# A post-norm decoder layer on one Trainium2 core: banks, splits and transposes in another order

## What is computed

```python
x = layernorm(x + gated_slot_attention(x, Wq, Wk, Wv, Wg, Ws, Wo, g_norm_weight))
x = layernorm(x + cross_attention(q=x, k=ctx_512, v=ctx_512))
g = (x @ gate_w.T) * gate_s          # [2048, 1408]
u = (x @ up_w.T) * up_s
x = layernorm(x + ((silu(g) * u) @ down_w.T) * down_s)
# gated slot attention, for each of 16 heads, 64 slots:
#   scores of each position on the slots (ok), pv = softmax(ok), o = pv against running slot values
#   o = rmsnorm(o) * weight * silu(x @ Wg); result = o @ Wo
```

## Time and profile before

| | us |
|---|---|
| median of three executions | 2014.69 |
| lowest and highest | 2011.48 and 2015.27 |
| the profiled execution | 2015.09 |
| its span | 2013.2 |
| PE busy | 1973.3 |
| DVE busy | 1367.3 |
| ACT busy | 778.5 |
| POOL busy | 562.7 |

### The profile page before, as it was taken

One profiled execution on the slowest core, in us unless ns is written; L12 is line 12 of the kernel. 1 busy time (PEld: TensorE's weight loads), 2 busy tenths in 40 slices (PEclk: granted clock), 3 DMA queues, 4 the chain that ended last, 5 costly groups with the idle time before them and its releaser, 6 DMA issues. The chain is left out here.

```text
span 2013.2 us, 30663 instructions
## 1 busy us (share of the span) xinstructions
PE 1973.3 (98%) x11850; PEld 1438.2 (71%) x11850; DVE 1367.3 (68%) x2206; ACT 778.5 (39%) x1915; POOL 562.7 (28%) x600
## 2 busy tenths in 40 slices
PE   8999999999999999999999989999999999999998
PEld 7888878878878888788788864444444378888876
DVE  4666666666666666666666778999999755555556
ACT  3332232332322322323223325888888721111113
POOL 2142152152142242242143242343242111111112
PEclk9999999999999999999999988999999999999999
DMA  5000100100001001001000001111110100000002
GB/s 167 1 1 12 37 1 11 37 10 24 15 12 37 1 11 37 1 11 38 1 12 4 6 2 26 26 26 31 26 26 20 34 16 16 31 16 30 17 16 84
DMA packets 58449, 46.89 MB, mean 23 GB/s; under 512 B 14288, under 2 KB 47056, under 8 KB 58320
## 3 DMA queue, kind: packets, MB, share of 16 engines
q1 hardware_dynamic: 58320, 45.11, 7.6%
HBM read 32.78 MB, written 4.19 MB: 18 GB/s over the span
## 5 line engine op out<-in xcount | busy, mean ns | idle before, releaser
L1693 DVE TENSOR_REDUCE a_raw_qks<-a_ps 128x1 f32<-128x512 f32 x512 | 321.0, 682 | 18.3 <-PE a_ps L937 17.7
L1621 ACT ACTIVATE x_prob<-a_ps 128x512 f32<-128x512 f32 x512 | 280.0, 609 | 64.8 <-PE a_ps L959 63.3
L66 PE MATMUL a_ps<-a_vg_hi,a_xT_lo 128*128 128x512 f32 x512 | 205.0, 400 | 0.0
L68 PE MATMUL a_ps<-a_vg_hi,a_xT_hi 128*128 128x512 f32 x512 | 199.8, 390 | 0.0
L67 PE MATMUL a_ps<-a_vg_lo,a_xT_hi 128*128 128x512 f32 x512 | 199.6, 390 | 0.0
L1745 DVE SCALAR_TENSOR_TENSOR a_gate<-a_gate,a_ps 128x256 f32<-128x256 f32 x128 | 53.8, 420 | 179.8 <-ACT a_gate L1509 179.8
L772 POOL TENSOR_TENSOR a_causal<-a_causal,a_mask 128x128 f32<-128x128 f32 x32 | 14.6, 458 | 561.7 <-ACT a_causal L1514 561.7
L66 PE MATMUL a_ps<-a_xT_hi,a_qks_lo 128*128 128x512 f32 x384 | 157.5, 410 | 0.4 <-DVE a_xT_lo L1724 0.4
L68 PE MATMUL a_ps<-a_xT_hi,a_qks_hi 128*128 128x512 f32 x384 | 150.5, 392 | 0.0
L67 PE MATMUL a_ps<-a_xT_lo,a_qks_hi 128*128 128x512 f32 x384 | 149.5, 389 | 0.0
L937 PE MATMUL a_ps<-a_xT_lo,a_xT_hi 64*128 64x512 f32 x384 | 143.8, 462 | 2.9 <-DVE a_raw_qks L1693 2.2
(11 more groups left out here) (202 smaller groups left out, 4588.8 us busy)
## 6 DMA issues: line engine op xcount, KB each, us to landing
a_raw_vg<-in_L_attn_Wv_dram SPq DMA_DIRECT2D x8, 512.0 KB, 4.1
a_raw_vg<-in_L_attn_Wg_dram SPq DMA_DIRECT2D x8, 512.0 KB, 6.9
a_raw_qks<-in_L_attn_Wo_dram SPq DMA_DIRECT2D x8, 512.0 KB, 3.7
a_xT_lo<-a_xT_lo SPq DMA_DIRECT2D x32, 128.0 KB, 2.3
x_values<-acc SPq DMA_DIRECT2D x13, 256.0 KB, 2.8
acc<-in_x_dram SPq DMA_DIRECT2D x3, 1024.0 KB, 10.4
out_dram<-acc SPq DMA_DIRECT2D x6, 512.0 KB, 2.8
f_raw_down<-in_L_ffn_down_w_dram SPq DMA_DIRECT2D x11, 256.0 KB, 3.0
```

The source lines that it names most:

```text
L66: pe.matmul(out, w_lo, x_hi, start=start, stop=False)
L68: return pe.matmul(out, w_hi, x_hi, start=False, stop=stop)
L1621: nc.scalar.activation(prob[par][:, s % 4, :], score_bank(q, s, par), ACT.Exp, scale=X_SCALE).then_inc(exp_done[par], 1)
L1693: nc.vector.tensor_reduce(nm[:, q % 2, i % 4, par, i // 4:i // 4 + 1], max_bank(u, q, i, par), AX.X, ALU.max, negate=True).then_inc(max_re ...
```

## The change

Nothing is added to or removed from the computation. Instructions change their places, and down tiles their banks.

- Attention, steps n = 2 to 30: `slot_softmax` is parted into `slot_maxima` and `less_maxima`; the addition of output tile 0 comes between them.
- Cross-attention's last unit: groups 9, 10, 11, 12, 13 go from turns 5, 7, 9, 11, 13 to turns 6, 8, 10, 13, 14; group 14 stays at 15.
- Entry: DVE's `inner(0, 0, 0)` comes ahead of the last batch's statistics; POOL's inverse deviation comes behind `low_h` of visit 0; in visit 1 the transposes of x stand behind the first half of `gate_up` and in the middle of the second one, not ahead of each, and wait for three and four additions instead of four; the wait for the sixteenth split stands ahead of down tile 2, not tile 0.
- Down banks: at b = 3 (chunks 0 to 7) tiles use `dnb[0], dnb[1], f_trb[1], dnb[0]`, so that tile 2 waits for no addition, and tile 3 for that of tile 0. Visit 36 uses four banks. Visit 35 stays with two.
- At b = 2 DVE adds tiles 0 and 1, then makes both gate and up rests, then adds 2 and 3; before, the rests stood ahead of tile 1 and tile 2.
- Chunks 9 and 10: the down weights are rounded (ACT) and their rest made (DVE) at the start of the visit, not behind `high_h` and `inner`.

```diff
+        def at_end(v):
+            return isinstance(v, int) and v == PAIRED - 1
         def down_bank(v, b, t):
-            four = v > PAIRED if paired(v) else b < 2
-            return f_trb[t - 2] if four and t >= 2 else dnb[t % 2]
+            if (paired(v) or b < 2) and t >= 2:
+                return f_trb[t - 2]
+            if b == B - 1 and not paired(v) and not at_end(v):
+                return (dnb[0], dnb[1], f_trb[1], dnb[0])[t]
+            return dnb[t % 2]
+        def early_down(next_down):
+            return isinstance(next_down, int) and next_down >= IC - 2
...
-            return {0: 5, 1: 6, 3: 7, 4: 8}.get(s, 7 + s // 2 if s % 2 else None)
+            return {0: 5, 1: 6, 3: 7, 4: 8, 6: 9, 8: 10, 10: 11, 13: 12, 14: 13, 15: 14}.get(s)
...
-            norm.inverse_deviation(pool, 0, 2 * B - 1)
             def visit(v, c, b, c1, b1, next_gu, next_down):
                 low_h(v, b)
+                if isinstance(c, int) and c == 0 and b == 0:
+                    norm.inverse_deviation(pool, 0, 2 * B - 1)
...
             def gate_up(v, c, b, x_batch=None):
+                wait(pe, h_ready, v - 1)
+                pe.wait_ge(gu_lo_ready, 2 * c + 1)
+                half_inner(v, c, b, 0)
                 if x_batch is not None:
                     f_transpose_x(x_batch, (0, 1))
                 pe.wait_ge(gu_lo_ready, 2 * c + 2)
-                wait(pe, h_ready, v - 1)
-                for w in range(2):
-                    if w == 1 and x_batch is not None:
-                        f_transpose_x(x_batch, (2, 3))
-                    half_inner(v, c, b, w)
+                half_inner(v, c, b, 1, range(KT // 2))
+                if x_batch is not None:
+                    f_transpose_x(x_batch, (2, 3))
+                half_inner(v, c, b, 1, range(KT // 2, KT))
...
-            def project_down(v, c, b, next_chunk=None):
+            def project_down(v, c, b, next_chunk=None, x_splits=None):
...
-                    if paired(v) and v > PAIRED + 1:
+                    if t == 2 and x_splits is not None:
+                        pe.wait_ge(f_xlo_ready, x_splits)
+                    if paired(v) and v > PAIRED:
                         pe.wait_ge(f_added, 4 * v + t - 3)
-                    elif paired(v):
-                        if v == PAIRED or t < 2:
-                            pe.wait_ge(f_added, 4 * v + t - 1)
-                    elif b >= 2 or b == 0 and t < 2:
-                        wait(pe, f_added, 4 * v + t - (3 if b == 2 and t < 2 else 1))
-                    elif b == 1:
+                    elif paired(v) and t < 2:
+                        pe.wait_ge(f_added, 4 * v + t - 1)
+                    elif paired(v) and t == 2:
+                        pe.wait_ge(down_lo_ready, IC)
+                    elif at_end(v):
+                        pe.wait_ge(f_added, 4 * v + t - 1)
+                    elif not paired(v) and b == B - 1 and t != 2:
+                        pe.wait_ge(f_added, 4 * v + (1 if t == 3 else t - 1))
+                    elif not paired(v) and b == 2:
+                        pe.wait_ge(f_added, 4 * v + t - (3 if t < 2 else 1))
+                    elif not paired(v) and b == 0 and t == 0:
+                        wait(pe, f_added, 4 * v)
+                    elif not paired(v) and b == 1:
                         pe.wait_ge(f_added, 4 * v + t - 3)
...
             def f_transpose_x(b, tiles):
                 if 0 in tiles:
                     pe.wait_ge(norm.done, TT * 2 * B)
-                    pe.wait_ge(f_added, TT)
                 for k in tiles:
+                    if k < 2:
+                        pe.wait_ge(f_added, k + 3)
...
             def visit(v, c, b, c1, b1, next_gu, next_down):
                 if isinstance(c, int) and c == 0 and b == 1:
                     f_high_x(B - 1)
+                if early_down(next_down):
+                    high_down(next_down)
...
+                if not (at(n, 0) or at(n, 1)):
+                    less_maxima(n)
+                if not first:
+                    add_out(n, (j - 1) % B, (1,))
...
             def add_out(v, b, next_chunk=None):
                 for t in range(TT):
-                    if next_chunk is not None and t in (1, 2):
-                        low_gu(next_chunk, (t - 1,))
+                    if next_chunk is not None and t == 2:
+                        low_gu(next_chunk)
...
+            inner(0, 0, 0)
             dve.wait_ge(x_added, 2 * UNITS)
             norm.statistics(B - 1, 0)
             dve.wait_ge(norm.stats_ready, 2 * B)
             norm.aggregate(0)
-            inner(0, 0, 0)
...
+                if early_down(next_down):
+                    low_down(next_down)
                 if c1 is not None:
                     inner(v + 1, c1, b1)
-                if next_down is not None and next_gu is not None:
-                    low_down(next_down)
                 if c1 is None:
                     add_last(v, b)
                 else:
                     add_out(v, b, next_gu)
-                if next_down is not None and next_gu is None:
+                if next_down is not None and not early_down(next_down):
                     low_down(next_down)
```

More of the change, by code:

```diff
@@ L1341, in gate_up, with half_inner @@
                 pe.wait_ge(gu_lo_ready, 2 * c + 2)
-                wait(pe, h_ready, v - 1)
-                for w in range(2):
-                    if w == 1 and x_batch is not None:
-                        f_transpose_x(x_batch, (2, 3))
-                    half_inner(v, c, b, w)
-            def half_inner(v, c, b, w):
-                for k in range(KT):
+                half_inner(v, c, b, 1, range(KT // 2))
+                if x_batch is not None:
+                    f_transpose_x(x_batch, (2, 3))
+                half_inner(v, c, b, 1, range(KT // 2, KT))
+            def half_inner(v, c, b, w, ks=range(KT)):
+                for k in ks:
                     mm = mm3(pe, gub[side(v, b)][w],
@@ L1352, in half_inner @@
                              (xT_hi[:, k, b * T:(b + 1) * T], f_xT_lo[:, k, b * T:(b + 1) * T]), k == 0, k == KT - 1)
-                mm.then_inc(gu_done, 1)
-            def project_down(v, c, b, next_chunk=None):
+                if KT - 1 in ks:
+                    mm.then_inc(gu_done, 1)
+            def project_down(v, c, b, next_chunk=None, x_splits=None):
                 pe.wait_ge(down_lo_ready, c + 1)
@@ L1451, in visit @@
                     pe.wait_ge(avn_ready, 2 * UNITS)
-                if first and b == 1:
-                    pe.wait_ge(f_xlo_ready, B * KT)
-                project_down(v, c, b, next_gu)
+                project_down(v, c, b, next_gu, B * KT if first and b == 1 else None)
             each_visit(pe, visit)
@@ L1674, in visit @@
                     high_h(v + 1, b1)
-                if next_down is not None:
+                if next_down is not None and not early_down(next_down):
                     high_down(next_down)
-                    if next_gu is not None:
-                        high_gu(next_gu)
+                if next_gu is not None and next_down is not None:
+                    high_gu(next_gu)
                 if paired(v) and c == LAST and b:
@@ L1808, in normalised_slots, with slot_maxima @@
                 nc.vector.tensor_tensor(okn, okb, rz[:, :], ALU.mult).then_inc(okn_ready, 1)
-            def slot_softmax(n):
+            def slot_maxima(n):
                 dve.wait_ge(ok_done, n + 1)
@@ L1813, in slot_softmax, with less_maxima @@
                 nc.vector.tensor_reduce(mx[:, :], scores, AX.X, ALU.max).then_inc(mx_ready, 1)
+            def less_maxima(n):
+                scores = tb.rearrange("p (g m) -> p g m", m=DK)
                 dve.wait_ge(mx_ready, n + 1)
@@ L1855, in step @@
                 gating(n + 1, VG + 1, b1)
-                slot_softmax(n)
+                slot_maxima(n)
+                if at(n, 0) or at(n, 1):
+                    less_maxima(n)
                 if at(n, 0):
@@ L1862, in step @@
                 if not first:
-                    add_out(n, (j - 1) % B, (0, 1))
+                    add_out(n, (j - 1) % B, (0,))
+                if not (at(n, 0) or at(n, 1)):
+                    less_maxima(n)
+                if not first:
+                    add_out(n, (j - 1) % B, (1,))
                 if at(n, 1):
```

## The result

| | before | changed |
|---|---|---|
| median | 2014.66 us (4 runs, 2011.48 to 2015.27) | 1993.07 us (4 runs, 1991.38 to 1994.07) |
| profiled execution, its span | 2015.09 us, 2013.2 us | 1993.76 us, 1991.9 us |
| mean granted clock | 0.993 | 0.994 |

A forecast was written before the change was run, and what follows sets the result against it. TensorE, busy 98% of the span, was taken as the bound, so only its waits and what follows them could be saved. 6.7 + 1.9 + 3.4 + 6.6 = 18.6 us off 2015.09 gave 1996.5 us, range 1992.5 to 2000.0.

The forecast's parts named there:

- Attention: Attention steps 2 to 29: output tile 2's wait for the addition of tile 0 goes, 28 x 0.24 = 6.7 us.
- the slack: Attention: the exponential, ending later, still leaves 2.0 us ahead of its transposes.
- Last unit: Cross-attention's last unit: four pairs of turns lose their group behind the odd turn; gain 1.9 us, between 1.2 and 2.3.
- Entry: Feed-forward entry: transposes of x to down projection takes 7.7 us, not 11.15; gain 3.4 us, bounds 1.0 to 4.0.
- Down projections: Down projections: waits at b = 3, b = 2 and in visits 35 and 36 shrink or go; 6.6 us, between 4 and 7.
- b = 3: Down projections, chunks 0 to 7: tile 2's wait is gone with the other bank, 0.42 + 7 x 0.37 = 3.0 us.
- the rests at b = 2: Down projections: the addition of tile 1 starts sooner, 9 x 0.09 = 0.8 us; tile 3 still waits about 0.25 us.
- early splits: Visit 35: down weights split at the visit's start remove most of a 2.35 us wait, gaining 2.4 us.
- 1: Attention's wait only moves, as later exponential or row sums delay the next stage: 6.7 us lost, 2003.2 us; chance 0.07.
- 4: Attention: late softmax makes TensorE wait for itself, slower than before, 2019 us and more; chance 0.02.
- 3: Down projections: the banks do nothing and early weights are held, 6 of 6.6 us lost, 2002.5 us; chance 0.04.
- Rival 2: Entry: the clock falls again behind the small waits, entry gains only 1.0 to 1.8 us, 1998.5 us; chance 0.07.

The follow-up runs named there:

- experiment 4: Changed kernel with the entry's TensorE order put back, then VectorE's and GpSimd's order, then both: 1994.84, 1991.01 and 1997.07 us.
- experiment 2: Changed kernel with attention's subtraction of the maxima moved behind both additions in steps 2 to 29: 1993.91 us.
- experiment 6: Changed kernel with one down-projection edit undone each time: banks at b = 3, early splits in visit 35, rests at b = 2: 1996.70, 1993.79, 1994.87 us.
- unit_undone: Changed kernel with the last unit's groups put back behind odd turns: 1994.03 us.
- third_bank: Changed kernel with output tile 3 at b = 2 of chunks 0 to 7 moved to the up half's already read bank: 1992.56 us.

## Why the prediction was right, point by point

*The whole.* 1996.5 us was forecast within 1992.5 to 2000.0, 1993.07 measured. On the profiled executions 18.6 stands against 21.3 us. The 2.7 us are: attention 1.4, last unit 0.5, entry 0.1, down projections 0.4, and 0.5 - 0.2 from start and stage, which the change doesn't touch. So every term came out larger than forecast, and no miss made up for another. The median lies near the lower end of the range: two of the four executions (1991.38 and 1992.38) are below 1992.5.

*Attention*, 6.7 forecast, 8.1 measured (7.7 undone). The mechanism and the slack (2.0 forecast, 1.96 seen) were right; the price of a wait was mis-sized. The prediction took the first two distances less 0.23 and 0.24 (0.17 + 0.07 us). Matmul by matmul against the changed kernel's trace, the mean over the 28 waits is 0.254 us for these two, because without a wait they are 0.226 and 0.227, and 0.039 us more for the nine behind them, which run at 0.228 to 0.235 us. That is 0.293 us, or 8.2 in 28 steps, where the table has 8.1 for the whole stretch. The upper bound, 28 x 0.25, was too low for that reason. (That VectorE is free at 709.84 does not follow from its row, which ends at 709.90; as tile 0 is done only at 709.98, nothing hangs on it.)

*Last unit*, 1.9 forecast, 2.3 measured: the two things set against it (a copy on ScalarE that might not fit, the last splits) cost nothing. It is the upper bound as the prediction had it.

*Entry*, 3.4 forecast, 3.5 measured: 2.63 us for line 144 where 2.62 had been worked out, two small waits, a clock of 1.00. The clock's part was 1.5 us, not 1.6. But the edit was taken as one; by experiment 4 the order of VectorE and GpSimd is a loss inside it, which the prediction could have seen: it had the additions 1.3 us later against TensorE than before. Trainium skill, GPSIMD Engine Reference, section Specifications: contention is with VectorE instructions in a two-port mode or with two inputs from SBUF. The trace agrees on both sides: line 144, with input and output in SBUF, is stretched (2.63 and 3.62 us for 1.92), while the four additions, one of whose inputs is in PSUM, take 2.47 us with GpSimd's `low_h` beside them. That line 144 runs in a two-port mode no run here shows.

*Down projections*, 6.6 forecast, 7.0 measured: b = 3 3.27 for 3.0, the rests at b = 2 1.16 for 0.8, early splits 2.2 for 2.4. At b = 3 it is again the slower pace behind a wait, 0.02 to 0.04 us each time. At b = 2 it is 0.95 us in nine visits, and visit 35, which has the same pattern and was not counted, gives 0.21. The early splits fall short by the new wait for GpSimd's scaling, which the prediction did not see.

*Rivals.* 1 and 4 fell with experiment 2, 3 with experiment 6. Rival 2, the clock at the entry, did not happen: with the two small waits (0.26 and 0.09 us) it stayed at 1.00 in all eight traces that have them (the changed kernel's and those of the runs that leave the entry alone). Behind pauses of 2 to 3 us the clock's answer was not the same each time.

## What to carry to other kernels

Where one engine is busy 98%, undo a change part by part and compare the start of the n-th matmul in two traces: effects of 0.4 us were read that way, where medians of one kernel move by 2. Price a wait by the time over which the rhythm is disturbed, not by its gap, and before a wait is removed look at what stands just behind it: of 0.37 us saved at one bank more than half went to a wait for the next. An edit with two halves on two engines needs two experiments.

## What the runs showed of the hardware

A restart of TensorE behind a wait costs 0.08 us (attention, 0.307 for 0.227) to 0.11 us (down projections, 0.337) in the next distance and 0.02 to 0.04 us more over the seven to nine behind it. At the passage from attention to the second attention, where TensorE is busy 69.0 to 69.6 of the 80 us from 1160 to 1240, the same instructions took up to 4.6 us more or less from one execution to the next; the granted clock of those 80 us was 0.91 in unit_undone (2.68 us shorter than the changed kernel's) and 0.85 in third_bank (1.77 longer):

```profile
1160.00:1240.00 80.00, 69.46 (x394) 0.91 0.06 13
```

```profile
1160.00:1240.00 80.00, 69.53 (x368) 0.85 0.06 13
```

The time goes with the granted clock in all fourteen profiled executions. At 0.85 (two of them) the stage is 1.8 us longer than in the changed kernel's, at 0.87 (five, that one among them) within 0.2 us of it, at 0.89 (two) 0.7 and 1.2 us shorter, at 0.91 (five) 2.0 to 2.8 us shorter. What makes the clock differ there is not shown. Among the profiled executions this passage differs more than any other that no edit touches, and it would be the next place to look.
